# A nine-stage kernel on one core: the convolution stage as one pipelined block, and the head loop flat with its last pass apart

## The chip, the cores and the metric

The kernel runs as one launch on one core of a Trainium2 chip. Its time is the device time of that launch in microseconds (us); the figure is the median of several runs. All arithmetic is float32, with matmul operands split into a high and a low float32r part where precision asks for it.

## What is computed

The input is 4 images of 128 channels by 32x32 (1024 tokens each). The reference runs six layers with residuals:

```python
x = _L0_conv_ref(x, ...)                 # non-local block, then batch norm
x = x + _L1_conv_ref(_gn(x), ...)        # group norm, 3x3 convolution with mixed experts
t = _to_tokens(x)
t = t + _L2_attn_ref(_ln_t(t), ...)
t = t + _L2_ffn_ref(_ln_t(t), ...)
t = t + _L3_attn_ref(_ln_t(t), ...)      # 16 heads, three branches
t = t + _L3_ffn_ref(_ln_t(t), ...)
```

Three of them matter here.

- `_L0_conv`: three 1x1 projections (theta, phi, g), the product `theta^T phi g / n` (reassociated, so only a 64x64 matrix is formed), a projection back, batch norm over all images, and the residual.
- `_L1_conv`: average pooling to 16x16, a small DCT and two small layers give for every image 8 mixing weights; the 3x3 kernel of an image is the weighted sum of 8 expert kernels (128x128x9); it is convolved with the group-normed image.
- `_L3_attn`: for each of 16 heads, causal attention over 1024 tokens, attention over 256 selected tokens, and attention in a window of 64; the three are gated, added and projected.

## The kernel before

The program runs the stages one after the other: a block that loads constants and casts masks, then `stage_conv` (L65), attention, feed-forward, latents, `stage_heads` (L2072), and the last feed-forward. Each stage is made of blocks: in a block every engine has its own instruction list, they meet only at semaphores, and all engines leave the block together.

**`stage_conv`** has two blocks. In the first, SyncE loads the weights and the four images (L140 to L143), TensorE takes one image after the other through projections (L178), the 64x64 product (L183), two small matmuls (L187 to L190) and the output (L194, whose result ScalarE copies to `WY` and VectorE takes statistics of); each step has one buffer, so that TensorE waits after most steps for VectorE or ScalarE. Then comes the batch norm: `bn_aggr` (L225), five small operations, and over the four images `WY = WY*scale + shift` (L234), `X = X + WY` (L238) and statistics for the group norm (L241). The group norm writes the padded images `XP` (L259). In the second block VectorE pools (`pr` L383, `pp` L385), ScalarE rounds `XP` to its high part (L347) and GpSimd subtracts it to get the low part `XPL` (L335). After transposes and small layers the mixing weights are ready, and VectorE mixes each image's kernel `KD` of 9 taps, 1152 columns, in 8 operations (L404 once, L406 seven times); ScalarE rounds it (L366), GpSimd subtracts (L341), TensorE does 54 matmuls (L316), and VectorE adds the result to `X` (L376). `hold_clock` (L1013) is 60 matmuls whose results nobody uses, ahead of the first convolution. At the end TensorE transposes `X` into token order (L327) and ScalarE copies that to `T` (L369).

**`stage_heads`** runs 16 passes, one for each of 4 images by 4 groups of 4 heads. The work of a pass is written out as the table `ORDER` (L1864 on): each word is a step such as `score.4.1` or `add.25`, and each engine runs those of its steps in the order of the table. A step with a `+` belongs to the *next* pass: it is done ahead. Before the loop the `+` steps run once alone for pass 0. `Count` and `Plan` work out the semaphore value that a step waits for; in a loop it is a register, computed from the pass number. On TensorE, VectorE, ScalarE and GpSimd the passes are two nested loops (images, head groups); on SyncE there are three loops, the last for the image that loads nothing further. In the last pass, the `+` steps run once more, on data that nobody uses.

The pass begins with `wk` (ScalarE rounds, L2492, VectorE subtracts, L2572). Then `tr.q2` and `tr.q3`: TensorE transposes two parts of the queries (L2288), and `split.tr.q2`, `split.tr.q3`: ScalarE rounds each to `QH` (L2470), VectorE subtracts to `QL` (L2564). Only then comes `near.4.0` (L2320), the window scores of a block of tokens, which needs `q2` split; `near_scores` has nine unused matmuls ahead of this step (`keep_clock`, L2414). `near.6.0` needs `q3` split. The pass ends with `add.21` to `add.27` on GpSimd (sums over exponentials, L2229), `sum.5` on TensorE (L2400), `norm.5` on VectorE (L2604 to L2612), `ysum.5` on GpSimd (L2238), `project.5` on TensorE (L2407), and the residual (L2619). Among these stand `+` steps, `+norm.0` (L2604 to L2612 again) the last of them.

Of the kernel before, what the change touches and what calls it, by code (L numbers as in the profile page):

```python
# [15 lines left out]
NT = N // 128  # L16
# [3 lines left out]
E1 = 8  # L20
# [44 lines left out]
def stage_conv(nc, keep, P, T, ident, d):  # L65


    with ExitStack() as ctx:
# [5 lines left out]

        X = sb("X", [C, B * N])
# [48 lines left out]
        ld_first, ld_w, ld_e, zeroed = sem("ld_first"), sem("ld_w"), sem("ld_e"), sem("zeroed")  # L124
# [5 lines left out]
        var_ready, std_ready, bn_scale = sem("var_ready"), sem("std_ready"), sem("bn_scale")  # L130
        bn_done, dch = sem("bn_done"), sem("dch")
        gstat, ggrp, gvar, gstd = sem("gstat"), sem("ggrp"), sem("gvar"), sem("gstd")

        nld = 8
        with nc.Block() as block:
            @block.sync
            def _(sp):
                for dst, src in ((PG, d["pg_w"]), (PGb, d["pg_b"].broadcast_to([128, 2 * CI])), (thw, d["theta_w"]),
                                 (thb, d["theta_b"]), (wwT, d["w_wT"]), (vec, d["vec"])):
                    sp.dma_start(dst[:, :], src).then_inc(ld_first, 16)  # L140
                for b in range(B):
                    sp.dma_start(X[:, b * N:(b + 1) * N], d["x"][:, b * N:(b + 1) * N]).then_inc(ld_x[b], 16)
                sp.dma_start(EX[:, :, :].rearrange("p e n -> p (e n)"), d["experts"]).then_inc(ld_e, 16)  # L143

            @block.scalar
            def _(act):
                for dst, src in ((blk4, d["blk4"]),
                                 (wf1, d["w_f1"]), (bf1, d["b_f1"]), (wf2, d["w_f2"]),
                                 (bf2, d["b_f2"].broadcast_to([128, 1])), (wr1, d["w_r1"]), (br1, d["b_r1"]),
                                 (wr2, d["w_r2"])):  # L150
                    act.dma_start(dst[:, :], src).then_inc(ld_w, 16)

                for b in range(B):
# [11 lines left out]

            @block.gpsimd
            def _(pool):
                nc.gpsimd.memset(XP[:, :, :, :], 0.0).then_inc(zeroed, 1)

            @block.tensor  # L170
            def _(pe):
                pe.wait_ge(ld_first, 16 * 6)
                for b in range(B):
                    pe.wait_ge(ld_x[b], 16)
                    for h in range(2):
                        for t in range(4):
# [3 lines left out]
                        last.then_inc(pg_ready, 1)  # L180
                    pe.wait_ge(pg_biased, 2 * b + 2)
                    for t in range(NT):
                        last = nc.tensor.matmul(P[2][0:CI, 0:CI], PT[:, t, CI:], PT[:, t, 0:CI],  # L183
                                                start=(t == 0), stop=(t == NT - 1))
                    last.then_inc(kvt_ready, 1)
                    pe.wait_ge(kvt_copied, b + 1)
                    nc.tensor.matmul(P[3][0:CI, 0:C], KVT[:, :], wwT[:, :], start=True, stop=True).then_inc(m_ready, 1)  # L187
                    pe.wait_ge(m_copied, b + 1)
                    nc.tensor.matmul(P[5][:, 0:1], M[:, :], thb[:, :], start=True, stop=True)
# [2599 lines left out]
```

## Time and profile before

| | |
|---|---|
| median of 3 runs | 2710.51 us (2709.5 to 2711.89) |
| the profiled execution | 2713.5 us, its span 2711.1 us |
| mean granted TensorE clock | 0.937 of 2.4 GHz |
| busy: TensorE, VectorE, ScalarE, GpSimd | 89%, 68%, 53%, 48% of the span |
| convolution stage with the constants before it | 0 to 189.8 us |
| head stage, its passes | about 738 to 2537 us |

A busy share is an average over stages with different limits, so what bounds is read from the timeline of each stage. In a timeline row stand the start, the time until the group's last instruction ended, engine, line, operation, tiles and, in brackets, how long the engine had been idle before and what ended that. A granted clock of 1.0 is 2.4 GHz, 0.5 is 1.2 GHz.

### The profile page before, as it was taken

Reading aid. Unit: us, or ns where it says so; the run is one execution under the profiler, and the core shown is the slowest. Engines: PE = TensorE matmul, PEld = TensorE weight load, DVE = VectorE, ACT = ScalarE, POOL = GpSimd, SP = SyncE. Lnnn points to the kernel's source line nnn. Section 1 sums busy time; section 2 is a strip of 40 time slices with the busy share of each in tenths; the row PEclk is TensorE's granted clock in tenths of the full one; section 3 lists DMA queues with packets and bytes.
Section 4 is the critical chain, followed back from the end, with each engine's and each line's share of the span. In section 5 each row is a group of like instructions: output and inputs, shape, how many; then the busy total and the mean of one; then the engine's idle time right before and its main releaser. Section 6 shows DMA issues by size and latency. Waiting matters only on the chain. (4 is left out here: it accounts for less than half of the span.)

```text
span 2711.1 us, 52559 instructions
## 1 busy us (share of the span) xinstructions
PE 2402.8 (89%) x17007; PEld 1743.4 (64%) x17007; DVE 1848.4 (68%) x3647; ACT 1435.4 (53%) x2524; POOL 1311.8 (48%) x999
## 2 busy tenths in 40 slices
PE   5598996856799999999999999999999999999867
PEld 3366663544567767666676766767667666676656
DVE  2767764677486776867768677686775867767636
ACT  1114553333366657666576665766656666566323
POOL 0213782000246647456474573755736557475445
PEclk8698997866999999999999999999999999999779
DMA  3004210011432121111211202122021120211233
GB/s 115 1 6 94 58 38 9 1 46 58 102 96 48 35 52 36 44 34 38 52 36 43 54 17 53 36 44 56 15 52 36 44 56 15 52 36 44 73 111 106
DMA packets 85091, 131.69 MB, mean 49 GB/s; under 512 B 16224, under 2 KB 60768, under 8 KB 84624
## 3 DMA queue, kind: packets, MB, share of 16 engines
q1 hardware_dynamic: 81328, 123.16, 18.1%
q0 software_dynamic: 3024, 7.43, 0.9%
q8 instruction: 41, 0.67, 0.1%
q14 instruction: 42, 0.34, 0.0%
q10 hardware_dynamic: 656, 0.09, 0.0%
HBM read 63.49 MB, written 20.79 MB: 31 GB/s over the span
## 5 line engine op out<-in xcount | busy, mean ns | idle before, releaser
L2511 ACT ACTIVATE a_PT<-PS 128x512 f32<-128x512 f32 (+1 forms) x1111 | 588.6, 564 | 361.5 <-PE PS L2376 238.8
L2229 POOL TENSOR_TENSOR a_KT<-a_PT 128x256 f32<-128x256 f32 (+2 forms) x179 | 356.4, 2001 | 470.1 <-ACT a_PT L2511 461.0
L2580 DVE TENSOR_REDUCE a_NM<-PS 128x2 fp32r<-128x512 f32 (+2 forms) x528 | 300.0, 612 | 146.6 <-PE PS L2320 83.1
L2229 POOL TENSOR_TENSOR a_KT<-a_KT,a_PT 128x2048 f32<-128x2048 f32 (+3 forms) x128 | 392.0, 3062 | 8.8
L2370 PE MATMUL PS<-a_QH,a_K 128*128 128x512 f32 (+3 forms) x768 | 292.1, 390 | 0.0
L2592 DVE TENSOR_REDUCE a_MX<-PS 128x1 f32<-128x512 f32 (+3 forms) x432 | 265.9, 665 | 32.7 <-PE PS L2335 18.1
L2370 PE MATMUL PS<-a_QH,a_KSW 128*128 128x192 f32 (+3 forms) x848 | 270.3, 340 | 12.1 <-DVE a_NM L2580 10.4
L2335 PE MATMUL PS<-a_K,a_QH 128*128 128x512 f32 (+3 forms) x768 | 252.3, 404 | 9.4 <-DVE a_K L2567 8.0
L2371 PE MATMUL PS<-a_QL,a_K1B 76*128 76x512 f32 (+3 forms) x768 | 259.3, 348 | 0.0
L2320 PE MATMUL PS<-a_KSW,a_QH 128*128 128x256 f32 (+2 forms) x1056 | 205.8, 307 | 4.1 <-DVE a_QL L2564 4.1
L2320 PEld LDWEIGHTS PS<-a_KSW,a_QH 128*128 128x128 f32 x1056 | 170.2, 194 | 50.5 <-DVE a_NM L2580 19.5
L2217 POOL TENSOR_TENSOR a_TM<-a_R 128x128 f32<-128x128 f32 x306 | 131.8, 457 | 136.8 <-DVE a_R L2546 136.8
L2567 DVE TENSOR_TENSOR a_KSW<-PS,a_KSW 64x512 fp32r<-64x512 f32 x170 | 117.2, 690 | 114.9 <-ACT a_KSW L2470 111.6
L2370 PEld LDWEIGHTS PS<-a_QH,a_KSW 128*128 128x128 f32 x848 | 164.2, 194 | 42.4 <-DVE a_NM L2580 14.3
L2470 ACT ACTIVATE a_QH<-PS 64x512 fp32r<-64x512 f32 x264 | 156.4, 593 | 43.8 <-PE PS L2288 38.9
L2376 PE MATMUL PS<-masks,identb 128*128 128x128 bf16 (+3 forms) x599 | 174.5, 291 | 0.0
L2370 PEld LDWEIGHTS PS<-a_QH,a_K 128*128 128x128 f32 x768 | 148.6, 193 | 26.8 <-issue 13.4
L2335 PEld LDWEIGHTS PS<-a_K,a_QH 128*128 128x128 f32 x768 | 135.6, 193 | 44.9 <-DVE a_MX L2592 17.3
L2497 ACT ACTIVATE a_QL<-PS 12x1024 fp32r<-12x1024 f32 x130 | 132.2, 1017 | 59.8 <-PE PS L2350 57.4
L2546 DVE TENSOR_TENSOR a_R<-PS,a_angles 128x512 f32<-128x512 f32 x153 | 102.3, 687 | 76.7 <-ACT a_TM L2462 75.6
L2371 PEld LDWEIGHTS PS<-a_QL,a_K1B 76*128 76x128 f32 x768 | 146.5, 191 | 9.7
L2371 PE MATMUL PS<-a_QL,a_KWB 76*128 76x192 f32 (+2 forms) x592 | 145.0, 275 | 0.0
(431 smaller groups left out, 5312.1 us busy)
## 6 DMA issues: line engine op xcount, KB each, us to landing
a_KWB<-a_KSW SPq DMA_DIRECT2D x68, 256.0 KB, 3.3
a_K1B<-a_K SPq DMA_DIRECT2D x32, 512.0 KB, 5.4
a_XC<-latents SPq DMA_DIRECT2D x17, 512.0 KB, 3.8
a_CKS<-latents SPq DMA_DIRECT2D x17, 512.0 KB, 4.6
a_CF<-latents SPq DMA_DIRECT2D x17, 448.0 KB, 4.2
slots<-in_empty_slots SPq DMA_DIRECT2D x1, 5160.0 KB, 18.7
f_XB<-slots SPq DMA_DIRECT2D x8, 645.0 KB, 4.8
c_EX<-in_experts SPq DMA_DIRECT2D x1, 4608.0 KB, 17.8
```

Of the source, the lines that this page charges most:

```text
L2217: last = nc.gpsimd.tensor_tensor(TM[:, x, :, 32 + c:48 + c], r[:, :, 0, c:c + 16], r[:, :, 1, other:other + 16], ALU.add)
L2229: nc.gpsimd.tensor_tensor(total, one_in, other_in, ALU.add).then_inc(s["added"], 1)
L2320: last = nc.tensor.matmul(bank[:, m * w:(m + 1) * w], QH[:, h, i * 128:(i + 1) * 128], keys[x][:, h, c0:c0 + w], start=m == 0, stop=x == 1 ...
L2335: last = nc.tensor.matmul(bank[:, m * w:(m + 1) * w], QH[:, h0 + m, i * 128:(i + 1) * 128], K1[:, h0 + m, c0:c0 + w], start=m == 0, stop=n ...
L2370: nc.tensor.matmul(out, keys[x][:, h, c:c + 128], QH[:, h, start:start + w], start=m == 0, stop=False)
L2371: last = nc.tensor.matmul(out, upper[x][0:DH + ROWS, h, c:c + 128], QL[0:DH + ROWS, h, start:start + w], start=False, stop=mask is None an ...
L2376: last = nc.tensor.matmul(by_heads[:, :, 0:cols], identb[:, :], add[:, None, :].broadcast_to([128, each, cols]), start=False, stop=True)
L2470: last = nc.scalar.activation(odd_even({"q": QH, "w": KW, "s": KS}[g[0]], e, rows, tokens(g)), ring(key)[e * DH:(e + 1) * DH, :].rearrange ...
L2497: nc.scalar.activation(QL[DH:DH + ROWS, :, p * PAIR:(p + 1) * PAIR], turning(key)[DH:DH + ROWS, None, 0:PAIR].broadcast_to([ROWS, QUAD, PA ...
L2511: nc.scalar.activation(PT[:, to:to + width], turning(key)[:, 0:width], ACT.Exp).then_inc(s["taken"], 1)
L2580: nc.vector.tensor_reduce(NM[:, i, DH:].rearrange("p (h x) -> p h x", x=3)[:, h:h + 2, x], ring(key)[:, 0:2 * w].rearrange("p (h n) -> p h ...
L2592: nc.vector.tensor_reduce(out, ring(key)[:, 0:heads * w].rearrange("p (h n) -> p h n", h=heads), AX.X, ALU.max, negate=True).then_inc(s["r ...
```

## The change

The block of constants is gone, and `stage_conv` has one block.

```diff
-        with nc.sbuf_tensor("maskf", [128, 7, 128], F32) as maskf, nc.Block() as block:
...
+                sp.dma_start(PG[:, :], d["pg_w"]).then_inc(ld_first, 16)
                 for b in range(B):
                     sp.dma_start(X[:, b * N:(b + 1) * N], d["x"][:, b * N:(b + 1) * N]).then_inc(ld_x[b], 16)
+                sp.dma_start(ident[:, :], d["ident"]).then_inc(ld_c, 16)
...
+                pe.wait_ge(warm_set, 1)
+                for _ in range(9):
+                    nc.tensor.matmul(P[7][:, :], warm[:, 0:128], warm[:, :], start=True, stop=True)
+                project(0)
+                project(1)
+                gram(0)
+                project(2)
+                middle(0)
+                gram(1)
+                weight(0)
+                project(3)
...
```

The other weights are loaded from ScalarE's queue. The images go through the projections staggered, with buffers of their own. In the batch norm one `scalar_tensor_tensor` per image makes `X = WY*scale + X`; the shift is added to the group norm's mean and, in `add_conv`, to `X`. Padding, `pr` and `pp` run image by image. The group norm's statistics and the mixing weights are worked out as before. GpSimd makes `XPL` once all four images are pooled, and its subtraction of the expert kernels goes to VectorE. The casts of the masks follow the pooling on VectorE. 36 unused matmuls stand ahead of the transposes of `pp`, 30 ahead of the first convolution.

```diff
+CHUNKS = ((0, 4), (4, TAPS))
...
+                pool.wait_ge(pooled, B)
+                for b in range(B):
+                    pool.wait_ge(image_high, b + 1)
...
+                for k, (b, n) in enumerate(jobs):
+                    if b >= 2 and n == 0:
+                        dve.wait_ge(kernel_low, len(CHUNKS) * (b - 1))
...
+                        if e == 2 and k:
+                            low_kernel(k - 1)
+                    ins.then_inc(mixed, 1)
+                    if b and n == len(CHUNKS) - 1:
+                        add_conv(b - 1)
```

The order of VectorE's mixing shows it: `KD` is the mixed kernel, `KDL` its low part, `KDH` its high part. Before:

```order
L399 TENSOR_TENSOR c_lg<-c_lg,c_lm 128x32
L404 TENSOR_SCALAR c_KD<-c_EX,c_lg 128x1152
L406 SCALAR_TENSOR_TENSOR c_KD<-c_EX,c_lg,c_KD 128x1152 x7
L404 TENSOR_SCALAR c_KD<-c_EX,c_lg 128x1152
L406 SCALAR_TENSOR_TENSOR c_KD<-c_EX,c_lg,c_KD 128x1152 x7
```

And now, on the same engine:

```order
L483 TENSOR_TENSOR c_lg<-c_lg,c_lm 128x32
L503 TENSOR_SCALAR c_KD<-c_EX,c_lg 128x512
L505 SCALAR_TENSOR_TENSOR c_KD<-c_EX,c_lg,c_KD 128x512 x7
L503 TENSOR_SCALAR c_KD<-c_EX,c_lg 128x640
L505 SCALAR_TENSOR_TENSOR c_KD<-c_EX,c_lg,c_KD 128x640 x2
L496 TENSOR_TENSOR c_KDL<-c_KD,c_KDH 128x512
L505 SCALAR_TENSOR_TENSOR c_KD<-c_EX,c_lg,c_KD 128x640 x5
```

Each image's kernel comes in two chunks of 4 and 5 taps, and VectorE subtracts the one while it mixes the next.

In `stage_heads` three rows of `ORDER` differ, and every engine has one loop of 15 passes; pass 15 follows it, written out with constants, without the `+` steps (`left_out`).

```diff
-wk tr.q2 tr.q3 split.tr.q2 split.tr.q3
+wk
 score.4.0
-score.4.1 v.v1.0 near.4.0
+score.4.1 v.v1.0 near.4.0 tr.q3 split.tr.q3
...
-+score.3.0 +rope.w3 +v.vw.1 +rope.q2 ysum.5 +v.vs.0 +tr.w3 +split.tr.w3 +a.q3 +rot.q3 +double.w3 project.5 +value.0.0 +value.1.1 +value.2.2 +add.0 +add.1 +value.3.3 +add.2 +add.3 +add.4 +add.5 +add.6 +sum.0 +rope.q3 +norm.0
++score.3.0 +rope.w3 +v.vw.1 +rope.q2 ysum.5 +v.vs.0 +tr.w3 +split.tr.w3 +a.q3 +rot.q3 +tr.q2 +split.tr.q2 +double.w3 project.5 +value.0.0 +value.1.1 +value.2.2 +add.0 +add.1 +value.3.3 +add.2 +add.3 +add.4 +add.5 +add.6 +sum.0 +rope.q3 +norm.0
...
+                with nc.Fori(0, FINAL, engines=[pe.engine], hint_back_edge=True) as q:
+                    one_pass(q % NQ, q)
+                one_pass(FINAL % NQ, FINAL)
...
-                    if i == 4 and n == 0:
-                        keep_clock(9, bank)
```

TensorE at the start of a pass in the loop, before (`a_TM` are queries to transpose, `a_QH`, `a_KSW` scores, `masks` the unused matmuls, the last row `near.4.0`):

```order
L2288 MATMUL PS<-ident,a_TM 128x128 x4
L2129 ISA
L2288 MATMUL PS<-ident,a_TM 128x128 x4
L2129 ISA x2
L2370 MATMUL PS<-a_QH,a_KSW 128x512
L2371 MATMUL PS<-a_QL,a_KSW 128x512
L2129 ISA
L2370 MATMUL PS<-a_QH,a_KSW 128x512
L2371 MATMUL PS<-a_QL,a_KSW 128x512
L2129 ISA x2
L2306 MATMUL PS<-a_WV,a_CF 128x128 x4
...
L2414 MATMUL PS<-masks,identb 128x384 x9
```

and now:

```order
L2478 MATMUL PS<-a_QH,a_KSW 128x512
L2479 MATMUL PS<-a_QL,a_KSW 128x512
L2242 ISA
L2478 MATMUL PS<-a_QH,a_KSW 128x512
L2479 MATMUL PS<-a_QL,a_KSW 128x512
L2242 ISA x2
L2416 MATMUL PS<-a_WV,a_CF 128x128 x4
L2242 REGISTER_ALU
L2428 MATMUL PS<-a_KSW,a_QH 128x256 x2
L2242 ISA
L2398 MATMUL PS<-ident,a_TM 128x128 x4
```

The transposes of `q2` left the start of the pass, those of `q3` stand behind `near.4.0` (L2428), and the unused matmuls are gone.

VectorE at the end of the loop now (`a_QL` is the split of `q2`, `T` the residual, the next three rows `+norm.0`, the last the branch back):

```order
L2675 TENSOR_TENSOR a_KSW<-PS,a_KSW 64x2x256 x2
L2242 REGISTER_ALU x2
L2654 TENSOR_TENSOR a_R<-PS,a_angles 128x512
L2242 REGISTER_ALU
L2672 SCALAR_TENSOR_TENSOR a_QL<-PS,a_QH 64x2x256 x2
L2242 REGISTER_ALU
L2727 ISA
L2727 TENSOR_TENSOR T<-T,PS 128x512
L2242 REGISTER_ALU x2
L2712 STREAM_TRANSPOSE a_RT<-PS 128x512
...
L2761 COMPARE_AND_BRANCH
```

The row of `a_QL` stood behind the branch before, as the second work of a pass; it is now ahead of the residual.

## Rows read from the trace of the kernel before

**Rows 1.** Table by stretches: start:end, length, busy us by engine, granted clock, DMA share, GB/s.

```profile
7.60:62.60 55.00, 35.36 (x168) 22.52 (x168) 13.70 (x28) 8.58 (x14) 3.95 (x1) 0.81 0.34 129
...
850.00:2500.00 1650.00, 1587.99 (x11652) 1141.12 (x11651) 1196.18 (x2015) 1039.26 (x1854) 951.24 (x734) 0.99 0.18 42
```

**Rows 2.** Timeline, start to first aggregate: start us, us, engine, line, operation, tiles, idle before.

```profile
0.75 0.39 SPq L2674 DMA_DIRECT2D ident<-in_ident  x1
...
10.98 1.86 SPq L142 DMA_DIRECT2D c_X<-in_x  x4
...
16.13 1.20 PE L178 MATMUL PS<-c_PG,c_X 128*128 128x128 f32 x4 [16.13 <-DMA c_X<-in_x]
...
62.66 0.37 DVE L225 BATCH_NORM_AGGREGATE c_mv<-c_st 128x2 f32<-128x48 f32 x1
```

**Rows 3.** Timeline, VectorE in the two normalizations.

```profile
64.27 2.98 DVE L234 TENSOR_SCALAR c_WY<-c_WY,c_sc 128x1024 f32<-128x1024 f32 x4
...
67.16 4.63 DVE L238 TENSOR_TENSOR c_X<-c_X,c_WY 128x1024 f32<-128x1024 f32 x4
...
79.94 2.98 DVE L259 TENSOR_SCALAR c_XP<-c_X,c_gmv,c_gq 128x1024 f32<-128x1024 f32 x4
```

**Rows 4.** Timeline, VectorE's pooling, then GpSimd in the same stretch.

```profile
83.45 0.69 DVE L383 TENSOR_TENSOR c_pr<-c_XP 128x512 f32<-128x512 f32 x1 [0.53 <-PEq L135]
...
87.90 3.10 DVE L383 TENSOR_TENSOR c_pr<-c_XP 128x512 f32<-128x512 f32 x1
...
96.82 0.43 DVE L385 TENSOR_TENSOR c_pp<-c_pr 128x256 f32<-128x256 f32 x1
...
84.68 11.56 POOL L335 TENSOR_TENSOR c_XPL<-c_XP,c_XPH 128x1156 fp32r<-128x1156 f32 x4 [73.13 <-ACT c_XPH L347]
```

**Rows 5.** Timeline, expert mixing: VectorE, then ScalarE's last copies.

```profile
112.89 0.82 DVE L404 TENSOR_SCALAR c_KD<-c_EX,c_lg 128x1152 f32<-128x1152 f32 x1
...
113.75 10.14 DVE L406 SCALAR_TENSOR_TENSOR c_KD<-c_EX,c_lg,c_KD 128x1152 f32<-128x1152 f32 x7
...
124.66 12.38 DVE L406 SCALAR_TENSOR_TENSOR c_KD<-c_EX,c_lg,c_KD 128x1152 f32<-128x1152 f32 x7
...
187.75 1.09 ACT L369 ACTIVATE T<-PS 128x512 f32<-128x512 f32 x2 [0.32 <-PE PS L327]
```

**Rows 6.** Answer for line L2492: durations (ns), first and last start (us); idle ended by issue.

```profile
L2492 ACT ACTIVATE a_WKH<-a_WK x16: 407/408/419, 737.9 to 2420.1; 128x256 fp32r<-128x256 f32 x16
...
  issue: 17.1, 3
```

**Rows 7.** Timeline, one start of a pass inside a batch: TensorE, ScalarE, VectorE.

```profile
1305.51 1.06 PE L2306 MATMUL PS<-a_WV,a_CF 112*128 112x128 f32 x8
...
1309.53 0.53 PE L2320 MATMUL PS<-a_KSW,a_QH 128*128 128x256 f32 x2
...
1304.30 4.84 ACT L2470 ACTIVATE a_QH<-PS 64x512 fp32r<-64x512 f32 x8 [2.84 <-PE PS L2288]
...
1306.75 1.39 DVE L2564 SCALAR_TENSOR_TENSOR a_QL<-PS,a_QH 64x512 fp32r<-64x512 f32 x2
...
1309.18 1.39 DVE L2564 SCALAR_TENSOR_TENSOR a_QL<-PS,a_QH 64x512 fp32r<-64x512 f32 x2 [1.04 <-ACT a_QH L2470]
```

**Rows 8.** Timeline, ScalarE at the starts of the fifth pass (new batch) and the sixth.

```profile
1190.45 0.42 ACT L2492 ACTIVATE a_WKH<-a_WK 128x256 fp32r<-128x256 f32 x1 [5.85 <-issue]
...
1301.05 0.41 ACT L2492 ACTIVATE a_WKH<-a_WK 128x256 fp32r<-128x256 f32 x1
```

**Rows 9.** Timeline, the last pass: GpSimd, then VectorE.

```profile
2493.43 4.57 POOL L2229 TENSOR_TENSOR a_KT<-a_PT 128x2048 f32<-128x2048 f32 x1 [2.11 <-ACT a_PT L2511]
...
2500.88 21.25 POOL L2229 TENSOR_TENSOR a_KT<-a_KT,a_PT 128x2048 f32<-128x2048 f32 x6
...
2526.29 1.28 POOL L2238 TENSOR_TENSOR a_YT<-a_YA,a_YB 128x512 f32<-128x512 f32 x1 [2.52 <-DVE a_YB L2612]
...
2535.55 0.69 DVE L2612 TENSOR_TENSOR a_YA<-PS,a_RT 128x512 f32<-128x512 f32 x1
```

More of the change, by code:

```diff
@@ L308, in _ @@
+                hold_clock(nc, P[7], ident, 30)
+                for k, (b, n) in enumerate(jobs):
                     pe.wait_ge(image_low, b + 1)
-                    pe.wait_ge(kernel_low, b + 1)
+                    pe.wait_ge(kernel_low, k + 1)
+                    first, end = CHUNKS[n]
                     for h in range(2):
-                        if b > 1:
+                        if b > 1 and n == 0:
                             pe.wait_ge(conv_added, 2 * (b - 2) + h + 1)
-                        for tap in range(TAPS):
+                        for tap in range(first, end):
@@ L314, in _ @@
                             dy, dx = divmod(tap, 3)
[L315 removed]
+                            for term, (kernel, image) in enumerate(((KDH, XPH), (KDH, XPL), (KDL, XPH))):
                                 last = nc.tensor.matmul(P[2 * (b % 2) + h][:, :], kernel[:, b % 2, tap * C:(tap + 1) * C],
                                                         image[:, b, 16 * h + dy:16 * h + dy + 16, dx:dx + HW],
[L318 removed]
@@ L372, in add_conv @@
-            def add_conv(nc, dve, b):
-                for h in range(2):
-                    k = b * N + h * HALF
-                    dve.wait_ge(conv_ready, 2 * b + h + 1)
-                    nc.vector.tensor_tensor(X[:, k:k + HALF], X[:, k:k + HALF], P[2 * (b % 2) + h][:, :], ALU.add)\
-                        .then_inc(conv_added, 1)
+                                                        start=(tap == 0 and term == 0), stop=(tap == TAPS - 1 and term == 2))
+                        if n == len(CHUNKS) - 1:
+                            last.then_inc(conv_ready, 1)
@@ new lines, in moments @@
+                def moments(b):
+                    for h in range(2):
+                        k = b * N + h * HALF
+                        dve.wait_ge(wy_copied, 2 * b + h + 1)
+                        ins = nc.vector.bn_stats(st[:, 2 * b + h, :], WY[:, k:k + HALF])
+                    return ins
+                dve.wait_ge(ld_first, 16 * 6)
+                add_bias(0)
+                add_bias(1)
+                keep_gram(0)
+                add_bias(2)
+                scale_middle(0)
@@ L2060, in all_of, with left_out @@
         _, count, times = self.sem[name]
-        return (passes * count.total + count.base) * times
+        return (passes * count.total + count.credit) * times
+    @staticmethod
+    def left_out(q, ahead):
+        return not ahead if q is None else ahead and isinstance(q, int)
     @staticmethod
     def before(events, key, q, same):
-        names = [name for name, early in events if early or q is not None]
+        names = [name for name, early in events if not Plan.left_out(q, early)]
         n = names.index(key)
+        passed = [name for name, _ in events] if q is not None else names[:n + 1]
         return next((name for name in names[n - 1::-1] if n and same(name)),
-                    next((name for name in names[:n:-1] if same(name)), None) if q is not None else None)
+                    next((name for name in passed[:passed.index(key):-1] if same(name)), None))
 def stage_heads(nc, keep, PS, P, T, ident, identb, masks, turned, latents, d, slots, emptied):
```

440 lines of the change are left out of this document (237 added, 203 removed).

## The prediction, as it was made before the changed kernel ran

> **What bounds the kernel now.** I read the page's busy shares first, then the table by stretches, since a share over the whole span mixes stages. In the long middle of the head stage TensorE is busy 1588 of 1650 us at a granted clock of 0.99 [rows 1]: there only time in which TensorE stands, or works for nobody, can be won. In the first 55 us of the convolution stage it is busy 35.36 us of 55 at 0.81 [rows 1]; the rest of that stage is a chain over all engines. So I went on to the timelines: the start [rows 2], the two normalizations [rows 3], pooling [rows 4], mixing [rows 5]; then the starts of the passes, by the one line that every pass begins with [rows 6] and in the timelines of one inner and one outer start [rows 7, 8]; last the end of the last pass [rows 9]. The reader is to see in each of them which engine's work is last and what stands idle for it.
>
> **Part A, the convolution stage.**
>
> *Start and projections.* The first image is asked for at 10.98, and the first projection runs at 16.13, 5.15 us later [rows 2]. Ahead of it lie the block of constants and six weight loads on the same queue. Now the image is the second load of the program's first block; the first load of the program went out at 0.75 [rows 2], so with 0.4 us for one load the image lands at about 6.3. Its masks and the expert kernels come behind it on the queue and are wanted later. The 35.36 us of TensorE at 0.81 are 28.6 at full clock [rows 1]. Staggered, a step of one image waits while another's runs, so I let TensorE go through and add 2 us for the last statistics: 6.3 + 28.6 + 2 = 37 for the first aggregate, which was at 62.66 [rows 2]: **-25.6**. If the clock stays at the 0.81 of before, it is 6.3 + 35.4 + 2 = 43.7, or -19.
>
> *Batch norm.* Scale-and-shift of four images and the addition take from 64.27 to 71.8 [rows 3], 7.5 us. One operation per image replaces them. The nearest row for it is the mixing operation of the same kind on 1152 columns, 10.14 / 7 = 1.45 us each [rows 5]; on 1024 columns 1.29, four of them 5.1, or **-2.5**. A shift of 0.2 us now runs behind the first of them.
>
> *Padding and pooling.* From the first padding at 79.94 to the end of the last pooling sum at 97.24 are 17.3 us [rows 3, 4], though four paddings are 2.98, and a pooling pair alone 0.69 + 0.43. The reason is in the rows: with GpSimd's four subtractions running (84.68 to 96.24) the same pooling operation takes 3.10 instead of 0.69 [rows 4]. GpSimd now waits for all four images, so the pairs cost what the first does: 2.98 + 4 x (0.69 + 0.43) + 0.8 for gaps = 8.3. I give 1 us back for the 36 unused matmuls ahead of the transposes: **-8.0**. The 11.56 us of subtractions move behind the pooling. From the last pooling sum to the first mixing operation are 112.89 - 97.24 = 15.65 us, so they are covered; the two casts lie in that chain's idle time too: if each waited for a whole subtraction (11.56 / 4 = 2.9), that is 5.8 us, still inside. The block switch and small waits give **-1.2**.
>
> *Mixing and convolution.* From 112.89 to the last copy's end at 188.84 are 75.95 us [rows 5]. VectorE mixes an image in 0.82 + 10.14 = 11.0 us undisturbed, and 2.2 more when GpSimd subtracts beside it (12.38) [rows 5], three times of four. In chunks an image costs more operations: I put seven of 512 columns at 0.79 and seven of 640 at 0.92, between proportional to columns (0.65, 0.81) and the price of the whole (1.45), with 0.52 and 0.59 for the firsts, 13.1 us; then two subtractions that were GpSimd's (1.6, from the 1.16 of an addition of 1024 columns [rows 3]) and two additions of results (1.2): 15.9 per image, 63.6 for four. Behind these stand the last chunk's rounding, 30 matmuls of the convolution (7.3) and the last turn: about 72.2 in all, because the turns of the first three images now lie between. **-3.7**, bounds -9 (proportional prices) and +4 (VectorE's waits for ScalarE uncovered).
>
> A is -25.6 - 2.5 - 8.0 - 1.2 - 3.7 = **-41**, bounds -28 and -47.
>
> **Part B, one loop in place of two.** Sixteen passes start from 737.9 to 2420.1 [rows 6], 15 intervals of 112.1 us on average; an inner one, from 1190.45 to 1301.05, is 110.6 [rows 8]. Together 23 us are lost against fifteen of these. The same answer says that ScalarE stood before this line three times, 17.1 us in sum, for nothing that the profile shows [rows 6]: the starts of passes 4, 8 and 12, where the loop over images turns (5.85 at the first [rows 8]). In the inner starts it goes on at once. ScalarE has 2.84 us of slack at such a start [rows 7], so three gaps cost at least 17.1 - 3 x 2.84 = 8.6 and at most 17.1; by the intervals I take 14. With one loop these starts are like inner ones: -14. Some of the other 9 us I take for dips of the clock after TensorE's waits; fewer waits, -4. The exit into the last pass may cost a gap of its own, 0 to 5.85: +3. **-15**, bounds -5 and -19.
>
> The row shows a gap at outer turns alone, at inner back edges none. The Trainium skill, "Runtime: NRT & Kernel Launch", section "Instruction fetch mechanics", says that a taken branch whose target is outside the two pages held forces a fetch before execution goes on. By it inner back edges should stop as well, since they return over a whole pass; the trace disagrees, and the time by that rule is the second rival's below.
>
> **Part C, the last pass without ahead work.** The end of the last pass is GpSimd's chain: from the sum at 2493.43 through one addition of results to the six sums that end at 2522.13 [rows 9]. Without the `+` steps TensorE reaches that first sum earlier: four projections, which I price by one of the same size, 1.06 [rows 7], and three transposes at half of that, are 5.8, less their overlap 4.9. GpSimd's own `+` step between is gone as well. The chain then takes 4.57 + 1.30 + 21.25 = 27.1 from 2488.5 and ends at 2515.6. From 2522.13 to the start of the last addition of results are 4.16 us [rows 9]; that addition takes 1.28, projection and residual some 2: 2523. The stage ended at 2536.24 with a normalization for nobody [rows 9]: -13.3. TensorE, which waits for GpSimd in that stretch, may lose its clock: +1.8. **-11.5**, bounds -5 and -15.
>
> **Part D, the start of a pass.** TensorE's own work ends at 1305.51 + 1.06 = 1306.57, and `near.4.0` starts at 1309.53 [rows 7]: 2.96 us of waiting and unused matmuls per pass. It waits for the split of `q2`, whose rounding starts at 1304.30 (eight operations for `q2` and `q3` together) and whose subtraction at 1306.75 [rows 7]. Both parts of `q2` now lie in the pass before. But the subtraction (1.39) goes into VectorE's row ahead of the residual and `+norm.0`, which moves by as much, to about 1307.8; `near.4.1` and its reduction stand behind it. The rounding of `q3` stays on ScalarE ahead of the exponentials, 2.4 us of the 4.84, and the subtraction at 1309.18 [rows 7] can come only little earlier; the scores' tiles are freed by exponentials and reductions behind these two. So of 2.96 I let 1.1 be won in each of 15 starts: **-16.5**. The bounds are nothing (VectorE and ScalarE keep the pace) and the whole 15 x 2.96 = -44.
>
> **The sum** is -41 - 15 - 11.5 - 16.5 = -84. Against the profiled execution of 2713.5 us that is 2629.5. It was 3.0 above the median of the runs, 2710.5, so the forecast is **2626.5**.
>
> **The rivals.**
> 1. *The projections stay at a low clock.* For it: 0.81 in that stretch, and a wait between nine first matmuls and the first image. Against it: denser work. Aggregate at 43.7 or, lower still, 49: +7 to +12, 2636.
> 2. *Every back edge of the long loop stops ScalarE*, as the outer ones do. This is the one that ends slower. The loop has 14 turns; with p us lost at each, and the gain of D lost since the pass start waits for ScalarE anyway, the sum is -41 - 11.5 - 14 + 14p: nothing at p = 4.75, and with the whole gap of 5.85 [rows 8] it is +15.4, or 2726. For it: one loop now holds what two did. Against it: twelve inner turns over the same body stop nowhere [rows 6].
> 3. *The start of a pass gives nothing*, because VectorE's splits are merely moved: 2643. For it: VectorE's row at the start is full [rows 7].
> 4. *The start gives all of it*: 2599. For it: the middle is bound by TensorE [rows 1], so what is freed might be used.
> 5. *The staggering doesn't do what it says*: TensorE waits for VectorE's bias additions after each half image as before. Then the start alone gains 9.8 of 25.6: 2642.
>
> **How the numbers follow.** The forecast, within 10 us, has 0.57; rival 1 0.12, rival 2 0.03, rival 3 0.13, rival 4 0.10, rival 5 0.05. The range takes in rivals 1, 3, 4 and 5 and some of their sums: 2598 to 2650. About 0.2% (5.4 us) is what a measurement of this kernel can tell from no change. All but rival 2 are faster by far more: faster 0.97, and the 0.03 are split over p around and above 4.75 us: same 0.01, slower 0.02.
>
> **What would show it.** First projection near 6.3 and first aggregate near 37; no pooling operation above 0.75 us; from the first mixing operation to the last copy near 72; the next stage at about 149 instead of 190. Intervals between passes all alike, near 109.5, and no gap of ScalarE at an issue but at the loop's exit; nothing behind the last residual, some 13 us earlier than its pass ended before. An interval of 110.6 would mean rival 3, one of 108 rival 4, one above 114 rival 2. I am wrong as a whole if passes grow, or if mixing grows past 80 us.

## The result and the profile after

The changed kernel takes 2675.53 us (median of 4 runs, 2668.8 to 2686.62) against 2711.2 us before on the same chip: ratio 0.9866, 95% interval [0.9826, 0.9906]. It is faster, by 36 us where 84 were forecast, and the time lies above the range. Measured again beside later runs it took 2670.28 us, ratio 0.9841 [0.9825, 0.9858]. The profiled execution of the changed kernel took 2674.1 us, its span is 2672.0.

Where the two traces differ, stretch by stretch (us; a stretch ends where the next one's first work starts):

| stretch | before | after | difference | forecast |
|---|---|---|---|---|
| start to the attention stage | 189.8 | 147.5 | -42.3 | -41 |
| attention, feed-forward, latents, ahead work of the head stage | 548.1 | 557.8 | +9.7 | 0 |
| 15 intervals from pass to pass | 1682.2 | 1690.4 | +8.2 | -31.5 |
| last pass to the next stage | 117.0 | 106.2 | -10.8 | -11.5 |
| last stage | 174.0 | 170.1 | -3.9 | 0 |

So two of the four terms, A and C, came out within a microsecond and a half. Most of the miss is in the loop of passes, 39.7 us of it; another 9.7 stand between the convolution and the loop. Of these, 5.8 are in the attention stage (last run below) and 3.9 lie between it and the first pass: with `q2` split ahead, its split for pass 0 is done before the loop. In two kernels below that split `q2` at the start of a pass this stretch is as long as before (306.7 and 306.9 us, 306.7 before, 310.6 in the changed kernel).

**The convolution stage.** The timeline of the changed kernel, TensorE, VectorE, GpSimd, ScalarE, answers to [rows 2 to 5]:

```profile
1.32 3.82 PE L285 MATMUL PS<-c_warm 128*128 128x512 bf16 x9 [1.32 <-POOL c_warm L226]
...
10.68 0.58 PE L247 MATMUL PS<-c_PG,c_X 128*128 128x128 f32 x1 [5.53 <-DMA c_vec<-in_vec]
...
38.58 0.37 DVE L424 BATCH_NORM_AGGREGATE c_mv<-c_st 128x2 f32<-128x48 f32 x1
...
41.07 3.67 DVE L432 SCALAR_TENSOR_TENSOR c_X<-c_WY,c_sc,c_X 128x1024 f32<-128x1024 f32 x3
...
60.26 0.42 DVE L465 TENSOR_TENSOR c_pp<-c_pr 128x256 f32<-128x256 f32 x1
...
75.41 0.49 DVE L503 TENSOR_SCALAR c_KD<-c_EX,c_lg 128x512 f32<-128x512 f32 x1
...
75.94 5.48 DVE L505 SCALAR_TENSOR_TENSOR c_KD<-c_EX,c_lg,c_KD 128x512 f32<-128x512 f32 x7
...
98.51 4.56 DVE L505 SCALAR_TENSOR_TENSOR c_KD<-c_EX,c_lg,c_KD 128x640 f32<-128x640 f32 x5
...
60.77 10.80 POOL L233 TENSOR_TENSOR c_XPL<-c_XP,c_XPH 128x1156 fp32r<-128x1156 f32 x4 [55.58 <-ACT c_XPH L191]
...
145.97 0.60 ACT L211 ACTIVATE T<-PS 128x512 f32<-128x512 f32 x1 [0.47 <-PE PS L346]
```

The first projection runs at 10.68, not at the 6.3 of the forecast: all six weights are one semaphore, and `vec`, the last of them on ScalarE's queue, lands last. But with the staggering the rest is faster than I took it, so the aggregate comes at 38.58 (37 was forecast). Between the two TensorE is busy 26.03 of 27.90 us, at a granted clock of 0.92 (columns as in [rows 1]); rival 1 had it stay at 0.81:

```profile
10.68:38.58 27.90, 26.03 (x168) 19.00 (x168) 13.23 (x29) 6.58 (x13) 0.00 (x0) 0.92 0.43 171
```

The batch norm's operations are 3.67 us for three, the last pooling sum ends at 60.68, no pooling operation takes more than 0.69 us, and GpSimd's subtractions (10.80 us) run behind it. From the first mixing operation at 75.41 to the end of the last copy at 146.57 are 71.2 us (72.2). The chunk prices were 5.48 / 7 = 0.78 and 4.56 / 5 = 0.91 us (0.79 and 0.92). The attention stage's first work starts at 147.5 (149).

**The loop.** The line that answers to [rows 6]:

```profile
L2600 ACT ACTIVATE a_WKH<-a_WK x16: 417/417/418, 705.3 to 2395.7; 128x256 fp32r<-128x256 f32 x16
```

15 intervals in 1690.4 us are 112.7 each; there is no idle time by issue ahead of the line any more. The three long intervals that ended at an outer turn (116.2 to 116.7) are gone as forecast. But of the other twelve, 109.1 to 112.7 before, half were 110.6 to 110.8; now 13 of 15 are 112.3 to 113.0, and two 111.4. The timeline of a start with 111.4, TensorE, then VectorE, then ScalarE, which answers to [rows 7]:

```profile
1269.79 0.50 PE L2478 MATMUL PS<-a_QH,a_KSW 128*128 128x512 f32 x1
...
1272.11 0.51 PE L2478 MATMUL PS<-a_QH,a_KSW 128*128 128x512 f32 x1 [1.58 <-DVE a_RT L2712]
...
1273.82 0.60 PE L2398 MATMUL PS<-ident,a_TM 128*128 128x128 f32 x4
...
1276.11 0.34 PE L2432 MATMUL PS<-masks,identb 128*128 128x384 bf16 x1
...
1278.34 0.47 PE L2428 MATMUL PS<-a_KSW,a_QH 128*128 128x192 f32 x2 [1.89 <-DVE a_QL L2672]
...
1269.32 1.39 DVE L2672 SCALAR_TENSOR_TENSOR a_QL<-PS,a_QH 64x512 fp32r<-64x512 f32 x2 [0.58 <-ACT a_QH L2578]
...
1271.35 0.71 DVE L2712 STREAM_TRANSPOSE a_RT<-PS 128x512 f32<-128x512 f32 x1
...
1276.90 1.39 DVE L2672 SCALAR_TENSOR_TENSOR a_QL<-PS,a_QH 64x512 fp32r<-64x512 f32 x2 [2.07 <-ACT a_QH L2578]
...
1274.46 1.80 ACT L2578 ACTIVATE a_QH<-PS 64x512 fp32r<-64x512 f32 x3
```

The program writes transposes and scores into a few banks in turn (the ring), and lets TensorE write a bank again only when its last contents have been read. TensorE stands twice for such a bank. The second half of `score.4.0` (1272.11) waits 1.58 us for the `+norm.0` of VectorE, whose first operation has to read its bank (1271.35) and comes behind the split of `q2` (1269.32). Then near scores (1278.34) wait 1.89 us for the split of `q3`: transposed at 1273.82, rounded on ScalarE from 1274.46 for 2.41 us (its first three operations are the row shown), subtracted from 1276.90. Together TensorE stands 3.47 us. The 2.96 us that a start lost before were 1.62 of standing, in the row below of the kernel before, and 1.34 of the nine unused matmuls:

```profile
1308.19 1.64 PE L2414 MATMUL PS<-masks,identb 128*128 128x384 bf16 x9 [1.62 <-DVE a_QL L2564]
```

The groups of TensorE's instructions in the head stage say the same for all passes; at the end of a line stands the idle time just before the group, and what ended it:

```profile
L2478 PE MATMUL PS<-a_QH,a_KSW 128*128 128x192 f32 (+3 forms) x832 | 274.4, 351 | 37.9 <-DVE a_RT L2712 23.7 <-DVE a_NM L2688 10.5 <-DMA a_WP<-in_w_proj 2.0
...
L2428 PE MATMUL PS<-a_KSW,a_QH 128*128 128x256 f32 (+2 forms) x1024 | 203.6, 310 | 34.2 <-DVE a_QL L2672 34.2
```

34.2 us of waiting for `a_QL`, 4.0 of them ahead of the first pass, and 23.7 for `a_RT`, 16 passes: 1.9 and 1.5 us each. The table by stretches shows what the other 1.5 us of an interval are; after a start whose interval was 111.4 the clock stays at 1.00, and behind the next one it falls to 0.54:

```profile
1272.70:1382.20 109.50, 105.37 (x782) 75.80 (x780) 78.78 (x134) 70.29 (x126) 65.20 (x50) 1.00 0.17 37
...
1384.10:1387.50 3.40, 3.40 (x17) 3.24 (x17) 2.06 (x4) 1.36 (x3) 0.00 (x0) 0.54 0.16 48
```

Such stretches at 1.2 GHz stand behind 13 of the 15 starts in the loop, and behind two with the same waits there is none; before there were 7.

**The last pass**, GpSimd, TensorE, VectorE, answers to [rows 9]:

```profile
2463.77 4.55 POOL L2339 TENSOR_TENSOR a_KT<-a_PT 128x2048 f32<-128x2048 f32 x1 [2.99 <-ACT a_PT L2619]
...
2470.90 21.45 POOL L2339 TENSOR_TENSOR a_KT<-a_KT,a_PT 128x2048 f32<-128x2048 f32 x6 [1.35 <-ACT a_PT L2619]
...
2496.96 1.26 POOL L2348 TENSOR_TENSOR a_YT<-a_YA,a_YB 128x512 f32<-128x512 f32 x1 [4.61 <-DVE a_YB L2720]
...
2492.41 1.93 PE L2508 MATMUL PS<-a_KT,a_ones 128*32 128x512 f32 x8 [7.01 <-POOL a_KT L2339]
...
2500.39 0.69 DVE L2727 TENSOR_TENSOR T<-T,PS 128x512 f32<-128x512 f32 x1 [3.51 <-PE PS L2515]
```

The chain starts 5.3 us earlier against the start of its pass, the six sums end at 2492.35, and behind the residual (2501.08) nothing follows.

### The profile page after: what moved, and what is told of

Read it like the earlier page. It is cut to its first block and busy times, and to the rows that moved or that the text cites. A ratio compares the mean times of both kernels' runs of the same rounds, so it can differ in the third digit from the quotient of the medians.

```text
span 2672.0 us, 51289 instructions
## 1 busy us (share of the span) xinstructions
PE 2371.9 (89%) x16679; PEld 1723.8 (65%) x16679; DVE 1814.7 (68%) x3640; ACT 1418.3 (53%) x2489; POOL 1287.1 (48%) x972
## 5 line engine op out<-in xcount | busy, mean ns | idle before, releaser
L2619 ACT ACTIVATE a_PT<-PS 128x512 f32<-128x512 f32 (+1 forms) x1104 | 586.7, 564 | 420.5 <-PE PS L2484 241.4
L2688 DVE TENSOR_REDUCE a_NM<-PS 128x2 fp32r<-128x512 f32 (+2 forms) x512 | 291.7, 612 | 139.5 <-PE PS L2428 78.7
L2478 PE MATMUL PS<-a_QH,a_KSW 128*128 128x192 f32 (+3 forms) x832 | 274.4, 351 | 37.9 <-DVE a_RT L2712 23.7
L2428 PE MATMUL PS<-a_KSW,a_QH 128*128 128x256 f32 (+2 forms) x1024 | 203.6, 310 | 34.2 <-DVE a_QL L2672 34.2
L2428 PEld LDWEIGHTS PS<-a_KSW,a_QH 128*128 128x128 f32 x1024 | 167.1, 199 | 84.1 <-DVE a_QL L2672 38.8
L2327 POOL TENSOR_TENSOR a_TM<-a_R 128x128 f32<-128x128 f32 x288 | 124.0, 457 | 130.4 <-DVE a_R L2654 130.4
L2675 DVE TENSOR_TENSOR a_KSW<-PS,a_KSW 64x512 fp32r<-64x512 f32 x160 | 110.3, 689 | 108.2 <-ACT a_KSW L2578 105.2
L2654 DVE TENSOR_TENSOR a_R<-PS,a_angles 128x512 f32<-128x512 f32 x144 | 96.2, 686 | 73.0 <-ACT a_TM L2570 72.0
```

What stands on the lines that cost most here:

```text
L2327: last = nc.gpsimd.tensor_tensor(TM[:, x, :, 32 + c:48 + c], r[:, :, 0, c:c + 16], r[:, :, 1, other:other + 16], ALU.add)
L2428: last = nc.tensor.matmul(bank[:, m * w:(m + 1) * w], QH[:, h, i * 128:(i + 1) * 128], keys[x][:, h, c0:c0 + w], start=m == 0, stop=x == 1 ...
L2478: nc.tensor.matmul(out, keys[x][:, h, c:c + 128], QH[:, h, start:start + w], start=m == 0, stop=False)
L2619: nc.scalar.activation(PT[:, to:to + width], turning(key)[:, 0:width], ACT.Exp).then_inc(s["taken"], 1)
L2688: nc.vector.tensor_reduce(NM[:, i, DH:].rearrange("p (h x) -> p h x", x=3)[:, h:h + 2, x], ring(key)[:, 0:2 * w].rearrange("p (h n) -> p h ...
```

## The experiments

Theories for the loop: the *order theory* (the moved splits make TensorE wait) and the *clock theory* (the waits are no worse than before; without the unused matmuls the clock falls). For the rest: whether B's gain comes from the flat loop. All medians are of 4 to 7 runs, beside 8 to 10 of the kernel before on the same chip; the intervals are those of the 15 from pass to pass.

**Order as before.** In the changed kernel:

```diff
-wk
+wk tr.q2 tr.q3 split.tr.q2 split.tr.q3
...
-score.4.1 v.v1.0 near.4.0 tr.q3 split.tr.q3
+score.4.1 v.v1.0 near.4.0
...
+                    if i == 4 and n == 0:
+                        keep_clock(9, bank)
```

and `+tr.q2 +split.tr.q2` out of the last row.

> The changed kernel with the three rows of the order table as before and the nine unused matmuls ahead of near.4.0 back; the convolution, the flat loop and the last pass apart stay. Order theory (the moved splits cost the time): the intervals between passes fall from 112.9 to 110.7 us everywhere, three gaps of the outer turns stay away, and the time falls by about 15 x 2.2 = 33 us against the changed kernel, to about 2643. Loop theory (one long loop makes a pass longer, whatever its order): intervals stay near 113 and the time near 2675.

Measured: 2641.69 us (2639.76 to 2642.31), ratio 0.9745 [0.9725, 0.9765].

```profile
L2602 ACT ACTIVATE a_WKH<-a_WK x16: 407/408/417, 695.2 to 2360.7; 128x256 fp32r<-128x256 f32 x16
```

1665.5 us for 15 intervals, 110.7 to 110.8 in 12 of them. The long loop is no slower; the new order, with the unused matmuls gone, costs some 30 us (2670.28 or 2675.53 against 2641.69).

**The unused matmuls back, nothing else.** 

```diff
+                    if i == 4 and n == 0:
+                        keep_clock(9, bank)
```

> The changed kernel with nothing but the nine unused matmuls ahead of near.4.0 put back. Clock theory (the longer passes are those in which the granted clock fell to 0.5 at their start, because the unused matmuls are gone): the 13 dips go, intervals are 111.4 instead of 112.9, time about 2675 - 13 x 1.5 = 2655. Order theory (two new waits of TensorE at the start, for VectorE): the waits of 1.6 and 1.9 us stay or the matmuls only fill one of them, dips may still come, time between 2668 and 2690.

Measured: 2723.47 us (2703.83 to 2735.76), ratio 1.0041 [1.0011, 1.0071].

```profile
L2602 ACT ACTIVATE a_WKH<-a_WK x16: 416/417/417, 699.9 to 2440.3; 128x256 fp32r<-128x256 f32 x16
...
1285.12 2.20 PE L2524 MATMUL PS<-masks,identb 128*128 128x384 bf16 x9
...
1291.91 0.36 PE L2430 MATMUL PS<-a_KSW,a_QH 128*128 128x192 f32 x1 [1.90 <-DVE a_QL L2674]
```

Both theories missed the size: intervals are 116.0, with two stretches of low clock in each pass (the nine matmuls take 2.20 us in the row above). Neither wait is shorter (1.90 us for the split of `q3`), and the nine matmuls are added to the path. The clock theory, that they would save 20 us, falls.

**`q2` alone.** In the changed kernel `q3` goes back to the start, `q2` stays ahead:

```diff
-wk
+wk tr.q3 split.tr.q3
...
-score.4.1 v.v1.0 near.4.0 tr.q3 split.tr.q3
+score.4.1 v.v1.0 near.4.0
```

> The changed kernel with q2 split ahead, but q3 transposed and split at the start of the pass as before, no unused matmuls. If the split of q2 ahead of the residual is what costs (score.4.0 then waits for the bank that the ahead normalization still holds), that wait of 1.6 us stays, intervals 111.5 to 113, time 2660 to 2680. If the split of q3 behind near.4.0 costs (near.4.3 waits for it, 1.9 us), intervals fall to about 110 and the time to about 2635.

Measured: **2617.34 us** (2614.77 to 2618.09), ratio 0.9653 [0.9634, 0.9673].

```profile
L2600 ACT ACTIVATE a_WKH<-a_WK x16: 416/417/417, 700.3 to 2341.9; 128x256 fp32r<-128x256 f32 x16
...
L2478 PE MATMUL PS<-a_QH,a_KSW 128*128 128x192 f32 (+3 forms) x832 | 267.7, 343 | 16.9 <-DVE a_NM L2688 10.5 <-DVE a_RT L2712 3.2 <-ACT a_PT L2619 0.6
...
L2428 PE MATMUL PS<-a_KSW,a_QH 128*128 128x256 f32 (+2 forms) x1024 | 200.4, 306 | 4.0 <-DVE a_QL L2672 4.0
...
L2398 PE MATMUL PS<-ident,a_TM 128*128 128x128 f32 x576 | 87.9, 275 | 16.8 <-DVE a_QL L2672 13.6 <-DMA a_WP<-in_w_proj 2.2 <-DVE a_R L2654 1.0
```

Intervals are 109.4, all but the first. The near scores' wait for `a_QL` fell from 34.2 to 4.0 us, none of it in the loop, and that for `a_RT` from 23.7 to 3.2; the transposes of `q3` (L2398) wait 13.6 us for the split of `q2` instead. One stretch of low clock is left in the loop. The changed kernel differs from this one in the place of `q3` alone, so `q3` behind `near.4.0` costs 53 to 58 us. Against the order as before (2641.69) this kernel is 24 us faster, by two things at once: `q2` ahead, and the nine unused matmuls left out.

**`q3` alone.** `wk tr.q2 split.tr.q2` at the start, `q3` behind `near.4.0`, nothing ahead, no unused matmuls.

> The changed kernel with the third query group (q2) back at the start of the pass and only the fourth (q3) behind near.4.0; no unused matmuls. Late-split theory (transposes, 2.4 us of ScalarE and 1.4 of VectorE have only some 2.5 us of TensorE's work as cover before near.4.3 needs the bank): a wait of about 2 us for the split stays before near.4.2 or near.4.3, and the wait of near.4.0 for q2 comes back, intervals 112 to 115, time 2665 to 2700. Rival (the two parts only hurt together): intervals 110 to 111, time 2630 to 2645.

Measured: 2675.33 us (2671.59 to 2686.28), ratio 0.9873 [0.9845, 0.9901].

```profile
L2600 ACT ACTIVATE a_WKH<-a_WK x16: 407/407/417, 695.1 to 2390.3; 128x256 fp32r<-128x256 f32 x16
...
L2428 PE MATMUL PS<-a_KSW,a_QH 128*128 128x256 f32 (+2 forms) x1024 | 208.4, 316 | 47.1 <-DVE a_QL L2672 47.1
```

Intervals of 111.9 to 115.0. In the pass from 1264 us on, TensorE waits 1.95 us for `q2` ahead of `near.4.0` and 1.89 for the late `q3` behind it, so that wait comes without the early `q2` too. The kernel is 34 us slower than with the order as before, at a mean granted clock of 0.931 against 0.945. But it also lacks the nine unused matmuls of that kernel, and no run here has the order as before without them; how much of the 34 us is the late `q3` is therefore not shown.

**`q2` behind the ahead normalization**, at the end of the last row; `q3` behind `near.4.0`.

> The changed kernel with the transposes and split of q2 moved behind the ahead normalization, the last steps of a pass; q3 behind near.4.0 as in the changed kernel. The residual and the normalization are then not held up by the split (the wait of 1.6 us at score.4.0 goes), but near.4.0 waits for q2 as it did before. Late-split theory: the wait of 1.9 us for q3 stays in any case, so intervals 111.5 to 113.5, time 2650 to 2685. Rival (the first wait is what brings the dips): intervals near 110, time near 2630.

Measured: 2687.11 us (2683.12 to 2693.08), ratio 0.9896 [0.9869, 0.9924]; intervals 113.2 to 115.7.

```profile
L2600 ACT ACTIVATE a_WKH<-a_WK x16: 416/417/417, 704.0 to 2415.0; 128x256 fp32r<-128x256 f32 x16
...
1277.29 1.12 PE L2416 MATMUL PS<-a_WV,a_CF 112*128 112x128 f32 x6 [2.84 <-DVE a_QL L2672]
```

The wait for the normalization is gone, and in its place TensorE waits 2.84 us for a split at once; the later wait for `q3` is there too, but shorter (1.29 us in this pass). What is freed in one place is lost in the other. The time is 2 us above the range of the late-split theory, and its wait of 1.9 us did not stay as it was; the rival's 2630 is far off.

**`q3` a little earlier: behind `score.4.0`.** To test how the late split costs, its place alone is moved, with `q2` ahead:

```diff
-score.4.0
-score.4.1 v.v1.0 near.4.0 tr.q3 split.tr.q3
+score.4.0 tr.q3 split.tr.q3
+score.4.1 v.v1.0 near.4.0
```

> q2 split ahead as in the changed kernel; q3 transposed and split behind score.4.0, ahead of score.4.1, v.v1.0 and near.4.0. Cover theory (the chain of q3's transposes, 2.4 us on ScalarE, 1.4 on VectorE had too little TensorE work ahead of the near score that needs the bank): score.4.1, v.v1.0 and near.4.0 are about 2.1 us more of cover, the wait of 1.9 us goes, few dips, intervals 109.4 to 110.5, time 2617 to 2635. Rival (any place behind score.4.0 holds up ScalarE's exponentials): intervals 111 to 113, 2640 to 2675.

Measured: 2618.73 us (2617.53 to 2619.76), ratio 0.965 [0.9624, 0.9676].

```profile
L2600 ACT ACTIVATE a_WKH<-a_WK x16: 416/417/418, 700.0 to 2341.6; 128x256 fp32r<-128x256 f32 x16
...
L2478 PE MATMUL PS<-a_QH,a_KSW 128*128 128x192 f32 (+3 forms) x832 | 266.4, 341 | 24.4 <-DVE a_NM L2688 10.5 <-DVE a_RT L2712 10.2 <-DMA a_WP<-in_w_proj 2.0
...
L2428 PE MATMUL PS<-a_KSW,a_QH 128*128 128x256 f32 (+2 forms) x1024 | 200.5, 306 | 7.1 <-DVE a_QL L2672 7.1
```

Three TensorE steps more between the transposes and the near scores that need the bank, and the 1.9 us of waiting per pass are 0.2 (7.1 us less the 4.0 ahead of the first pass); intervals are 109.4.

**`q3` later: behind `near.4.3`.**

```diff
-score.4.1 v.v1.0 near.4.0 tr.q3 split.tr.q3
+score.4.1 v.v1.0 near.4.0
...
-score.5.0 +load.next near.4.1 near.4.2 near.4.3
+score.5.0 +load.next near.4.1 near.4.2 near.4.3 tr.q3 split.tr.q3
```

> q2 split ahead; q3 transposed and split still later, behind near.4.3, before near.5.0. Cover theory: ahead of the next near scores that need the bank stands only score.5.1, about 1 us, so the wait moves there and is 2 us or more; intervals 111.4 to 114 with dips of the clock, time 2650 to 2690. Rival (what is late for near.4.3 is simply moved out of the way, since only near.6.0 needs q3): no wait, intervals 109 to 110, time 2605 to 2625.

Measured: 2698.59 us (2696.53 to 2710.69), ratio 0.9951 [0.9922, 0.998]; intervals 113.4 and 115.3 by turns.

```profile
L2600 ACT ACTIVATE a_WKH<-a_WK x16: 416/417/418, 700.0 to 2415.4; 128x256 fp32r<-128x256 f32 x16
...
1280.68 0.66 PE L2398 MATMUL PS<-ident,a_TM 128*128 128x128 f32 x4
...
1285.25 0.47 PE L2428 MATMUL PS<-a_KSW,a_QH 128*128 128x192 f32 x2 [2.05 <-DVE a_QL L2672]
```

From the transposes to the near scores 4.57 us pass again, as in the changed kernel (1273.82 to 1278.34, 4.52), and TensorE has work for about half of them. The wait moves with the step. The time is 9 us above the range given, with 23 stretches of low clock in the loop where the changed kernel has 13. With the two places before, the waits and intervals bear out the cover theory, and both rivals' times are missed by more than 20 us.

**`q2` alone, with the unused matmuls.** 

> The version with q2 alone split ahead, with the nine unused matmuls ahead of near.4.0 put back. They are 1.35 us of TensorE at full clock, and nothing waits there now. If they only take their time: intervals 110.7, no dips, time about 2638. If such matmuls bring dips of their own, as the two per pass suggest where they were put back into the changed kernel: intervals above 112 with a dip in most passes, time above 2655.

Measured: 2631.93 us (2630.18 to 2633.47), ratio 0.9696 [0.967, 0.9722].

```profile
L2602 ACT ACTIVATE a_WKH<-a_WK x16: 416/417/418, 699.9 to 2355.4; 128x256 fp32r<-128x256 f32 x16
```

Intervals of 110.2: nine unused matmuls cost 0.9 us per pass and bring no fall of the clock where TensorE doesn't stand. So of the 24 us by which `q2` alone beats the order as before, some 12 to 15 are the matmuls left out (2631.93 less 2617.34 is 14.6; by the ratios, 0.9696 against 0.9653, it is 11.7) and the rest, some 10 to 13, is `q2` ahead.

**`q2` earlier.** In the version with `q2` alone, `+tr.q2 +split.tr.q2` ahead of `+tr.w3 +split.tr.w3`.

> The version with q2 alone split ahead, its transposes and split moved four steps earlier in the order, ahead of those of w3. It ended at 2617 with 0.9 us of waiting per pass for the split of q2 (the bank of tr.q3) and 0.2 for the ahead normalization. If the split comes about a microsecond earlier: intervals 108.5 to 109, time 2602 to 2612. If ScalarE's row only swaps two roundings and w3's is late instead: 109.4 or more, 2615 to 2640.

Measured: 2647.88 us (2646.63 to 2649.87), ratio 0.9763 [0.9746, 0.9779]; intervals 110.7 to 111.5 behind the first. It is 8 us above the second case: 30 us lost by four steps' difference. The trace shows the wait that took the place:

```profile
1261.91 0.65 PE L2398 MATMUL PS<-ident,a_TM 128*128 128x128 f32 x4 [2.54 <-POOL a_TM L2327]
```

ScalarE now rounds `q2` (2.39 us) ahead of `w3`, and VectorE's split of `q2` (1.39) stands ahead of its step `a_R` for `q3`. GpSimd's `a_TM`, made from that, comes later, and the transposes of `q3` at the start of the pass wait 2.54 us for it. What comes late is `q3`, not `w3` as the second case had it.

**The convolution alone.** The new `stage_conv` and what calls it, in the kernel before.

> The kernel before with the new convolution stage alone: old order, nested loops, last pass in the loop. The stage ends about 40.6 us earlier, as in the changed kernel. If the 5 us that the attention stage behind it lost in the changed kernel come from the new convolution's end, the time is 2711 - 41 + 5 = 2675; if they are chance of that execution, 2670. Both leave nothing for all the rest of the change but about 0 to 5 us.

Measured: 2655.97 us (2654.39 to 2657.68), ratio 0.9797 [0.9777, 0.9817], at least 14 us below either expectation. The line of [rows 6] in this kernel:

```profile
L2593 ACT ACTIVATE a_WKH<-a_WK x16: 409/409/418, 695.9 to 2362.1; 128x256 fp32r<-128x256 f32 x16
...
  issue: 1.6, 4
```

The loops are nested as before, yet the idle time of 17.1 us at the outer turns is 1.6. B's gain is here without B.

**Ten tiny copies on ScalarE.** In the kernel before, behind the group norm's square root:

```diff
+                act.wait_ge(gstd, 1)
+                for i in range(10):
+                    nc.scalar.activation(fill[:, i * B:(i + 1) * B], gr[:, :], ACT.Copy)
```

Until the first pass ScalarE executes 556 instructions in the trace of the kernel before, and 566 with the new convolution.

> The kernel before, with ten tiny copies more on ScalarE behind the group norm's square root, where it is idle for 3.7 us; nested loops and everything else as before. With the convolution alone the gaps of 5.85 us at the three outer turns were gone though the loops were still nested, and ScalarE's code stood ten instructions further on. Position theory (the gaps hang on where the loop's end lies in ScalarE's code): the line's idle by issue falls from 17.1 to about 1.6 us, the time by 12 to 16 us to about 2696. Rival (they vanished for another reason, the shorter convolution or its order): gaps as before, time 2710.

Measured: 2698.36 us (2695.8 to 2705.09), ratio 0.9957 [0.994, 0.9973].

```profile
L2496 ACT ACTIVATE a_WKH<-a_WK x16: 407/413/418, 738.3 to 2402.6; 128x256 fp32r<-128x256 f32 x16
...
  issue: 1.6, 4
```

Work was added, and 13 us are gone, though the loops are nested as before and the first pass starts 0.4 us later than it did. The stretches of low clock in the loop also fell from 7 to 2, so a part of the 13 us is the clock. What decides is thus not the nesting alone but what stands ahead of the loop in ScalarE's code; that it is the place of the loop's code is the likeliest reading, and only this one shift was made.

**The changed kernel once more.**

> The changed kernel once more, on the same chip as these. If the 5 to 6 us more in the attention stage and the spread of 2669 to 2687 belong to that kernel, they come again; in the four kernels with the same convolution that stage took 241.1 to 241.7 us, so I expect 2665 to 2675 and an attention stage of 241 to 247 us. Intervals between passes 111.4 or 112.9, as before.

Measured: 2670.28 us (2667.07 to 2677.39). Two of its intervals are 114.2 and 114.4, the others 111.4 to 113.0. Its attention stage took 243.2 us, after 247.2 in the first profile and 240.9 to 241.7 in nine other kernels here with the same convolution (245.0 in one, 241.4 in the kernel before). So most of the 6 us that this stage lost is no property of the new convolution; what brings it in some executions was not settled.

## Why the prediction was wrong

- **A** was right in sum (-41, measured -42.3) and in its parts, though the first projection came 4.4 us later than worked out of which the faster projections gave 2.8 back.
- **B** had the right size (-14 for three gaps) by luck, and the wrong reason. I ascribed them to two nested loops, as the rows allowed; the convolution alone and ten added copies take them away with the loops still nested, and with the flat loop on top 15 intervals only go from 1666.2 to 1665.5 us. The Trainium skill, "Runtime: NRT & Kernel Launch", section "Instruction fetch mechanics", has the stop depend on which pages of code are held when a branch is taken. I took it that by this the inner turns would stop as well, and set it aside since they don't. That step was not worked out: a pass is 277 to 282 instructions of ScalarE in the traces, and I did not hold this against the size of the two pages. A cost that goes with a shift of ten instructions agrees with the section, though no run here shows the pages.
- **C** was right: -10.8 of -11.5, by the chain that was named. The clock, which I put at +1.8, did fall: it was granted at 0.63 from 2485 to 2503 us, where before it was 1.00 over the last 15 us of the stage; its cost was not separated. That is not all: the last stage is 3.9 us shorter too. In the kernel before VectorE stood 2.70 us in that stage's norms for nothing that the profile shows, in the row below; the changed kernel has no such gap there. The two kernels above whose last pass stays in the loop (the convolution alone, the ten copies) have it too, 2.42 and 2.87 us, and none with the last pass apart; what makes it was not tested.

```profile
2548.54 0.87 DVE L1408 BATCH_NORM_STATS2 f_ln_st<-T 128x6 f32<-128x128 f32 x4 [2.70 <-issue]
```

- **D** failed. The step was "The bounds are nothing (VectorE and ScalarE keep the pace) and the whole": it let no loss in, and passes grew (112.1 to 112.7 us), which was the prediction's own sign of being wrong as a whole. I priced the engines' work and not the chain with what covers it. A transposed group stands in a bank of the ring until VectorE has split it. Behind `near.4.0` the chain of 4.5 us, transposes, 2.41 of ScalarE, 1.39 of VectorE, has 2.3 us of TensorE's work beside it; at the start of the pass it has enough: with `q2` alone no near score of the loop waits for a split. The rest of D held once `q3` doesn't undo it: -1.6 us per pass (24 us in 15), 0.9 of them the unused matmuls left out and 0.7 `q2` ahead. That this is near the 1.1 forecast is partly luck, for the 1.1 was picked between two bounds and not worked out. Rival 3 named VectorE's full row, but took it to cost the gain only.
- On top of the waits comes the clock, which I had put at -4 for fewer waits: TensorE stands twice within 9 us, and its clock was granted at 1.2 GHz behind 13 starts, some 1.5 us each. Against `q2` alone the waits are 2.0 us of a pass (111.4 against 109.4), and the low clock 1.5 more in most.

So the terms, from differences of medians: convolution -41 (an estimate: the -53.6 of the kernel with it alone, less the -12.8 of the ten copies, if its shift of ScalarE's code is worth the same), ScalarE's code moved -13, flat loop and last pass apart -14 (2655.97 to 2641.69), `q2` ahead with the unused matmuls left out -24, `q3` behind `near.4.0` +53 to +58.

## What to carry to other kernels

Before a step that fills a buffer is moved, write down the chain from filling to emptying and the work that the waiting engine has until it needs that buffer; a place three steps earlier made the difference between nothing and 55 us. When a move is bounded by "nothing", ask for the row that excludes a loss. Test the parts of a change one by one: here one phrase of the change was worth leaving out, and the others were worth 92 us together (2709.58 to 2617.34), some 13 of them by the unplanned shift of ScalarE's code.

## What the runs showed that was not expected

Ten copies added to an idle engine made the kernel 13 us faster, as the idle time by issue ahead of a pass fell from 17.1 to 1.6 us and the stretches of low clock from 7 to 2. And nine unused matmuls, put there to hold the clock, did not hold it: with TensorE waiting right beside them (`q3` late) they added 3.1 us per pass (112.9 to 116.0) and a second fall of the clock in each, without such waits 0.9 us and no fall.
